# Zero-padding the query block of each head to 128 rows for the score matmuls, and an fp32 matmul in place of a cast and a bf16 one

## The chip, the cores and the metric

One Trainium2 chip, 8 cores, each on 4 of the 32 sequences. There is no traffic between the cores. The metric is device microseconds of the slowest core. The profile names the engines PE (matrix), PEld (its weight loads), DVE (vector), ACT (scalar), POOL (GpSimd) and SP (DMA issue).

## The reference, cut to what matters

```python
def attn(x, Wq, bq, Wk, bk, Wv, bv, Wo, bo):      # 16 heads of 64, S = 2048, D = 1024
    q, k, v = ((x @ W + b).reshape(B, S, 16, 64).transpose(0, 2, 1, 3)
               for W, b in ((Wq, bq), (Wk, bk), (Wv, bv)))
    scores = einsum('bhqd,bhkd->bhqk', q, k) / sqrt(64)
    out = einsum('bhqk,bhkd->bhqd', softmax(scores, -1), v)
    return out.transpose(0, 2, 1, 3).reshape(B, S, D) @ Wo + bo

def ffn(x, w_gate, w_up, w_down):                 # hidden 3072, weights int * 1/127
    return (silu(x @ wg.T) * (x @ wu.T)) @ wd.T

x = x + layernorm(attn(layernorm(x), ...))
x = x + layernorm(ffn(layernorm(x), ...))
```

x is (32, 2048, 1024) in fp32.

## The kernel before

The program first casts and transposes the weights, and then goes through four sequences, one after the other. Each sequence has three stages: (A) layer norm, and the K, Q and V projections; (B) attention; (C) the feed-forward part in two halves. The change touches stage B alone.

In stage B, `K_fm` and `Q_fm` hold K and Q transposed: 128 partitions are two heads of 64, and head h lies in column block hc = h // 2 at partitions hr = 64 * (h % 2) onward. The unit of work is one head for one group of 512 queries: 64 units a sequence, unit u being group g = u // 16 and head h = u % 16. A unit walks the 2048 keys in 16 tiles of 128, taken as 8 pairs:

- two score matmuls (L479): weights are 64 rows x 128 keys of K, the moving operand is 64 rows x 512 queries of Q. They write a pair of PSUM banks; two such pairs alternate.
- one exponential on ACT (L486) over the 128x1024 pair, into one half of `Ebuf`. It is called exp below, exp0 to exp7 in a unit.
- two PV matmuls (L459): weights are 128 keys x 65 columns of V (64, and one of ones that sums the row), the moving operand is `Ebuf`. They run one pair late: PE's order is score 0, score 1, PV 0, score 2, PV 1, ..., score 7, PV 6, PV 7.

Then comes the normalisation. `plan_epi1` copies the row of sums to `srow` (L500, DVE; "the sums copy" below). `plan_epi2` takes Ln and Exp of it on ACT (L509, L511, giving `rs`), casts `rs` to bf16 (L514, DVE), spreads it over 64 partitions by a one-row matmul with a row of ones (L516, PE; "the spread"), copies the result out (L525, DVE) and multiplies the PV result by it into `attn_fm` (L527, DVE). `plan_epi2` of unit u-1 is emitted after the matmuls of unit u, and `plan_epi1` of u behind that. `rs_bf` lies in `gbf`, a buffer that the feed-forward stage uses too.

The order of everything is that of the code: `Plan.step` appends to a list, each engine runs its own steps of that list in order, and semaphore waits are written by hand. In units with index 1 to 8 of groups 1 to 3, half an output tile of the group before follows: `plan_otile` with 8 full matmuls (L546), a one-row bias matmul (L552) and a copy on ACT (L556). After each second half, in units of even index, `plan_ctile` follows: two layer norms of one 128-token tile, a chain that goes to and fro between DVE (L310 to L329, L575, L580, L587) and ACT (L323, L326). Of the 63 places where one unit follows another in a sequence, 12 hold half an output tile, 12 hold the other half and a `plan_ctile`, and 39 neither. The last group's output tiles come at the end of the stage.

Of the kernel before, what the change touches and what calls it, by code (L numbers as in the profile page):

```python
# [17 lines left out]
QSC = 1.0 / 127.0  # L18
SPREAD_OPROJ = True
PVLAG = True  # L20
E4BF16 = True


class PSem:
# [66 lines left out]
def build_program(truncate=None, truncate_at=None, debug_scratch=False):  # L91
# [43 lines left out]
    K_fm = AR[:, 0:16384]  # L135
    Q_fm = AR[:, 16384:32768]
# [33 lines left out]
    Wo_s = Wx[:, 8192:16384]  # L170
    gbf = sb("gbf", [128, 1024], BF16)
    rs_bf = gbf[0:1, 0:512]
    bstat = sb("bstat", [128, 12], F32)
    mvt = sb("mvt", [128, 2], F32)
    rst = sb("rst", [128, 1], F32)
# [13 lines left out]
    p = Plan()  # L189
# [3 lines left out]
    def rw(*names):  # L193
# [12 lines left out]
           inc=[(g_ev, 1)])  # L206
    p.step("gpsimd", lambda e: e.iota(coli, [[1, 128]], channel_multiplier=0,
                                      allow_small_or_imprecise_dtypes=True),
           inc=[(g_ev, 1)])
    p.step("vector", lambda e: e.tensor_tensor(ident_bf, ident_f, coli, ALU.is_equal),  # L210
           wait=[g_ev], inc=[(g_ev, 1)])
    p.step("vector", lambda e: e.tensor_tensor(ident_f, ident_f, coli, ALU.is_equal),
           wait=[g_ev], inc=[(g_ev, 1)])
# [4 lines left out]
    for nm, src, dstT in (("bq", BQ, bqT), ("bk", BK, bkT)):  # L218
        p.step("sync", lambda e, src=src: e.dma_start(
            out=bstg, in_=src.rearrange("(c p) -> c p", p=128)),  # L220
            wait=[(g_mm, g_mm.count)], inc=[(g_ld, 16)], tag=f"ldb_{nm}")
        p.step("tensor", lambda e: e.transpose(ps[:, 0:8], bstg, ident_f[0:8, 0:8]),
               wait=[g_ld, g_ev], inc=[(g_mm, 1)], tag=f"trb_{nm}")
        p.step("vector", lambda e, dstT=dstT: e.tensor_copy(dstT, ps[:, 0:8]),
               wait=[g_mm], inc=[(g_ev, 1)], tag=f"evb_{nm}")
    for nm, src, dst in (("bv", BV, bv_bf), ("bo", BO, bo_bf)):
        p.step("sync", lambda e, src=src: e.dma_start(
            out=brow, in_=src.rearrange("(a d) -> a d", a=1)),
            wait=[(g_ev, g_ev.count)], inc=[(g_ld, 16)], tag=f"ldr_{nm}")
        p.step("vector", lambda e, dst=dst: e.tensor_copy(dst, brow),  # L230
               wait=[g_ld], inc=[(g_ev, 1)], tag=f"cvr_{nm}")

    for nm, src in (("wq", WQ), ("wk", WK), ("wv", WV), ("wo", WO)):
        p.step("gpsimd", lambda e, src=src: e.dma_start(
            out=fstage[:, 0:8192], in_=src.rearrange("(c p) o -> p c o", p=128)),
            wait=[(g_st, g_st.count)], inc=[(g_ldg, 16)], tag=f"cast_{nm}")
        p.step("sync", lambda e, nm=nm: e.dma_start(
            out=wbf[nm].rearrange("(c p) o -> p c o", p=128), in_=fstage[:, 0:8192]),
            wait=[g_ldg], inc=[(g_st, 16)], tag=f"park_{nm}")
    for nm, src, dst in (("wg", WG, wg_bf), ("wu", WU, wu_bf), ("wd", WD, wd_bf)):  # L240
        p.step("gpsimd", lambda e, src=src: e.dma_start(
            out=fstage, in_=src.rearrange("(c p) o -> p c o", p=128)),
            wait=[(g_st, g_st.count)], inc=[(g_ldg, 16)], tag=f"cast_{nm}")
        p.step("sync", lambda e, dst=dst: e.dma_start(
            out=dst.rearrange("(c p) o -> p c o", p=128), in_=fstage),
            wait=[g_ldg], inc=[(g_st, 16)], tag=f"park_{nm}")

    for nm, srcs, dstT in (("wg", wg_bf, wgT_bf), ("wu", wu_bf, wuT_bf)):
        for c in range(8):
            for hg in range(6):  # L250
# [3 lines left out]
                    wait=[(g_st, g_st.count)], inc=[(g_lds, 16)], tag=f"xp_{nm}{c}_{hg}")  # L254
# [20 lines left out]

    lxs = [p.sem("lxa"), p.sem("lxb"), p.sem("lxc")]
    vns = p.sem("vns")
    lxi = [p.sem("lxia"), p.sem("lxib")]
    cs_x1 = [p.sem("csx1a"), p.sem("csx1b")]
    cs_l3 = [p.sem("csl3a"), p.sem("csl3b")]  # L280
# [22 lines left out]
    for s in range(NSEQ):  # L303
# [163 lines left out]
        def plan_unit(u):  # L467
            g, h = u // 16, u % 16
            hc, hr = h // 2, 64 * (h % 2)
            for jp in range(8):  # L470
                P = u * 8 + jp
                pr = P % 2
                for j in (2 * jp, 2 * jp + 1):
                    w = []
                    if j % 2 == 0:
                        w.append((sxp, max(0, sxp.count - 1)))
                    if u == 0 and j == 0:
                        w += builds_done
                    p.step("tensor", lambda e, j=j, pr=pr, hc=hc, hr=hr, g=g: e.matmul(  # L479
                        ps[:, 1024 * pr + 512 * (j % 2): 1024 * pr + 512 * (j % 2) + 512],  # L480
                        K_fm[hr:hr + 64, hc * 2048 + j * 128: hc * 2048 + (j + 1) * 128],
                        Q_fm[hr:hr + 64, hc * 2048 + g * 512: hc * 2048 + (g + 1) * 512],
                        start=True, stop=True),
                        wait=w, inc=([(smm, 1)] if j % 2 == 1 else []),
                        tag=f"s{s}sT{u}_{j}")
                p.step("scalar", lambda e, pr=pr: e.activation(  # L486
                    Ebuf[:, 1024 * pr:1024 * (pr + 1)],
                    ps[:, 1024 * pr:1024 * (pr + 1)], AF.Exp, scale=0.125),
                    wait=[(smm, smm.count), (pvm, pvm.count)],
                    inc=[(sxp, 1)], tag=f"s{s}xp{u}_{P}")  # L490
                if PVLAG:
                    if jp >= 1:
                        plan_pv_pair(u, jp - 1, sxp.count - 1)
                else:
                    plan_pv_pair(u, jp, sxp.count)
            if PVLAG:
                plan_pv_pair(u, 7, sxp.count)
# [345 lines left out]
```

How the kernel before makes its waits and increments, by code:

```python
            def body(eng):  # L66
                waited = {}
                for si, (engine, fn, waits, incs, tag) in enumerate(steps):
                    if engine != engine_name:
                        continue
                    for sm, val in waits:
                        if val > 0 and waited.get(id(sm), -1) < val:
                            eng.wait_ge(sm.handle, val)
                            waited[id(sm)] = val
                    inst = fn(eng)
                    self.emitted[si] = inst
                    if incs:
                        assert inst is not None, f"step {tag} needs inst for incs"
                        for sm, amt in incs:
                            inst = inst.then_inc(sm.handle, amt)
```

## Time and profile before

| what | us |
|---|---|
| median of 2 runs | 11290.91 |
| their range | 11266.82 to 11315.01 |
| the profiled execution's own time | 11263.55 |
| its span on the slowest core (core 7) | 11262.0 |
| spans of the eight cores | 11164.9 to 11262.0 |

The span runs from the first to the last instruction of the slowest core, and all rows below are of that core. Busy shares are means over stages with different limits, so the stage that the change touches has to be read by itself. PEclk is the clock that TensorE was granted, as a share of 2.4 GHz: 0.50 is 1.2 GHz, 1.00 is 2.4 GHz.

### The profile page before, as it was taken

To read this page: it belongs to the slowest core of one execution; us is meant where nothing else is said; L and a number is where in the kernel's file an instruction comes from. 1 tells how busy PE (TensorE), PEld (TensorE's weight loads), DVE (VectorE), ACT (ScalarE), POOL (GpSimd) and SP (SyncE) were. 2 spreads that over 40 slices of the span, in tenths; PEclk is the share of its full clock that TensorE was granted. 3 is DMA by queue.
4 is the path that set the end of the run, shared out by engine and by line. 5 is a ranking of instruction groups with operands and counts; after the bars stand their busy time and mean duration, and the time that the engine had idled before them with its cause. 6 is when DMAs were issued, how large, how long until landed. Compare 5 with 4: busy or idle time off the path is not lost.

```text
span 11262.0 us, 71264 instructions; the slowest of 8 cores (11164.9 to 11262.0 us)
## 1 busy us (share of the span) xinstructions
PE 7816.7 (69%) x22530; PEld 2125.4 (19%) x22530; DVE 3190.8 (28%) x5389; ACT 2811.4 (25%) x3601; POOL 335.0 (3%) x401
## 2 busy tenths in 40 slices
PE   0079888675648888866647988866575888886755
PEld 0031111122222111122212111112222211111222
DVE  0141221233352111234344122123335311122334
ACT  0005444300002444410000544430000244441000
POOL 0000000000000000000000000000000000000000
PEclk9985555587876555578877555558677655556767
DMA  9630000112131000012123000011213100001121
GB/s 194 155 109 0 19 14 14 47 40 77 53 101 49 10 14 14 19 57 63 56 79 101 0 19 19 10 47 45 71 42 107 54 10 12 17 19 54 40 71 62
DMA packets 300509, 558.30 MB, mean 50 GB/s; under 512 B 159842, under 2 KB 159858, under 8 KB 300148
## 3 DMA queue, kind: packets, MB, share of 16 engines
q0 software_dynamic: 81072, 287.34, 9.1%
q1 hardware_dynamic: 141508, 247.52, 6.6%
q10 hardware_dynamic: 77568, 18.89, 0.9%
q8 instruction: 195, 3.19, 0.1%
q14 instruction: 166, 1.36, 0.0%
HBM read 415.25 MB, written 130.02 MB: 48 GB/s over the span
## 4 chain that ended last, share of the span: by engine, by line
PE 57%; DVE 15%; DMA 10%; issue 7%; ACT 6%; ACTq 2%; SPq 2%; POOL 1%; DVEq 0%; POOLq 0%
PE ps L479 14%; PE ps L459 14%; PE ps L726 7%; PE ps L732 7%; DMA arena<-wdT_bf 4%; PE ps L397 4%; PE ps L679 4%; PE ps L546 4%; DVE arena L693 3%; PE ps L421 2%; DMA x1st<-x_s 2%; ACT rs L511 1%; ACT brow L509 1%; PE ps L516 1%; SPq L654 1%
## 5 line engine op out<-in xcount | busy, mean ns | idle before, releaser
L486 ACT ACTIVATE Ebuf<-ps 128x1024 bf16<-128x1024 f32 x2048 | 2069.1, 1023 | 2195.6 <-PE ps L479 2194.8
L459 PE MATMUL ps<-Ebuf,arena 128*65 128x512 bf16 x4096 | 2154.8, 628 | 655.9 <-ACT Ebuf L486 550.8
L726 PE MATMUL ps<-arena 128*128 128x512 bf16 x3072 | 1311.7, 427 | 1138.9 <-DMA arena<-wdT_bf 710.7
L479 PE MATMUL ps<-arena 64*128 64x512 bf16 x4096 | 2017.4, 606 | 6.5 <-DVE arena L434 6.5
L732 PE MATMUL ps<-arena 128*128 128x512 bf16 x3072 | 1305.2, 425 | 0.0
L514 DVE CAST gbf<-rs 1x512 bf16<-1x512 f32 x256 | 106.2, 415 | 3802.4 <-ACT rs L511 3802.4
L679 PE MATMUL ps<-arena 128*128 128x512 bf16 x3072 | 807.4, 394 | 184.0 <-DVE arena L693 147.8
L739 ACT ACTIVATE gbf<-ps 128x512 bf16<-128x512 f32 x384 | 229.3, 597 | 2823.9 <-PE ps L732 2823.8
L744 DVE SCALAR_TENSOR_TENSOR arena<-ps,gbf 128x512 bf16<-128x512 f32 x384 | 265.6, 692 | 2239.3 <-ACT gbf L739 2239.3
L362 PE MATMUL ps<-ident_bf,ln3st 128*128 128x128 bf16 x512 | 104.5, 266 | 1091.9 <-DVE ln3st L348 1026.1
L693 DVE SCALAR_TENSOR_TENSOR arena<-ps,arena 128x1024 f32<-128x1024 f32 x704 | 829.0, 1219 | 54.9 <-PE ps L679 26.6
L459 PEld LDWEIGHTS ps<-Ebuf,arena 128*65 128x65 bf16 x4096 | 382.7, 143 | 2357.3 <-issue 2357.3
L726 PEld LDWEIGHTS ps<-arena 128*128 128x128 bf16 x3072 | 329.7, 107 | 1628.5 <-issue 1419.6
L479 PEld LDWEIGHTS ps<-arena 64*128 64x128 bf16 x4096 | 295.5, 109 | 1471.6 <-issue 1458.8
L546 PE MATMUL ps<-Wx,attn_fm 128*128 128x512 bf16 x1024 | 435.3, 602 | 92.9 <-ACT o_tm L556 85.6
L397 PE MATMUL ps<-ln_bl,Wx 128*128 128x512 bf16 x2048 | 479.2, 398 | 13.2 <-DVE ln_bl L365 9.0
L732 PEld LDWEIGHTS ps<-arena 128*128 128x128 bf16 x3072 | 327.4, 107 | 439.6 <-issue 226.9
L679 PEld LDWEIGHTS ps<-arena 128*128 128x128 bf16 x3072 | 265.0, 98 | 711.9 <-issue 551.4
L705 POOL DMA_DIRECT2D arena<-wgT_bf x96 | 87.2, 909 | 8887.1 <-PE ps L479 5368.7
L516 PE MATMUL ps<-gbf,ones_bf 1*64 1x512 bf16 x256 | 153.5, 600 | 198.2 <-DVE gbf L514 198.2
L323 ACT ACTIVATE o_tm<-o_tm,epsv 128x1 f32<-128x1 f32 x64 | 18.8, 294 | 1056.7 <-DVE o_tm L316 1056.7
L362 PEld LDWEIGHTS ps<-ident_bf,ln3st 128*128 128x128 bf16 x512 | 52.2, 104 | 1146.3 <-issue 1137.7
(74 smaller groups left out, 3635.4 us busy)
## 6 DMA issues: line engine op xcount, KB each, us to landing
xin<-x SPq DMA_DIRECT2D x128, 512.0 KB, 4.2
arena<-wgT_bf POOLq DMA_DIRECT2D x96, 512.0 KB, 4.9
arena<-wuT_bf POOLq DMA_DIRECT2D x96, 512.0 KB, 5.8
arena<-wdT_bf POOLq DMA_DIRECT2D x96, 512.0 KB, 6.3
Wx<-wk_bf POOLq DMA_DIRECT2D x32, 1024.0 KB, 6.2
Wx<-wq_bf POOLq DMA_DIRECT2D x32, 1024.0 KB, 6.0
Wx<-wv_bf POOLq DMA_DIRECT2D x32, 1024.0 KB, 6.1
x_s<-x1st SPq DMA_DIRECT2D x64, 512.0 KB, 2.7
```

The lines of the kernel that those rows point to most:

```text
L397: p.step("tensor", lambda e, wsl=wsl, di=di, do4=do4, bk_i=bk_i: e.matmul(bank(bk_i), Wslot[wsl][:, di * 512 + do4 * 128: di * 512 + (do4 ...
L459: p.step("tensor", lambda e, j=j, pr=pr, u=u, h=h: e.matmul(ps[0:65, 2048 + 512 * (u % 2): 2048 + 512 * (u % 2) + 512], Vaug[:, j * 1040 + ...
L479: p.step("tensor", lambda e, j=j, pr=pr, hc=hc, hr=hr, g=g: e.matmul(ps[:, 1024 * pr + 512 * (j % 2): 1024 * pr + 512 * (j % 2) + 512], K_ ...
L486: p.step("scalar", lambda e, pr=pr: e.activation(Ebuf[:, 1024 * pr:1024 * (pr + 1)], ps[:, 1024 * pr:1024 * (pr + 1)], AF.Exp, scale=0.125 ...
L516: p.step("tensor", lambda e: e.matmul(ps[0:64, 3072:3584], ones_bf[0:1, 0:64], rs_bf[0:1, :], start=True, stop=True), wait=[epi], inc=[(ep ...
L546: p.step("tensor", lambda e, di=di, t4=t4, n=n, gb=gb: e.matmul(bank(7), attn_fm[:, gb + di * 512 + t4 * 128: gb + di * 512 + (t4 + 1) * 128],
L679: p.step("tensor", lambda e, c=c, n=n, tt=tt, hsl=hsl, fsl=fsl, dbk=dbk: e.matmul(bank(dbk + n), h_sfm[hsl][:, c * 1024 + tt * 128: c * 10 ...
L693: p.step("vector", lambda e, at=at, dbk=dbk: e.scalar_tensor_tensor(at, bank2(dbk), QSC, at, ALU.mult, ALU.add), wait=[(fdm, fdm.count)], ...
L726: p.step("tensor", lambda e, di=di, c=c, u2=u2, fsl=fsl, gbk=gbk: e.matmul(bank(gbk), wgT_s[fsl][:, di * 256 + c * 128: di * 256 + (c + 1) ...
L732: p.step("tensor", lambda e, di=di, c=c, u2=u2, fsl=fsl, ubk=ubk: e.matmul(bank(ubk), wuT_s[fsl][:, di * 256 + c * 128: di * 256 + (c + 1) ...
L739: p.step("scalar", lambda e, gbk=gbk, gsl=gsl: e.activation(gbf[:, gsl * 512:(gsl + 1) * 512], bank(gbk), AF.Silu, scale=QSC), wait=[(fmm, ...
L744: p.step("vector", lambda e, ubk=ubk, gsl=gsl, hsl=hsl, c=c, u2=u2: e.scalar_tensor_tensor(h_sfm[hsl][:, c * 1024 + u2 * 512: c * 1024 + ( ...
```

## The change

Before each unit, DVE now fills one half of `gbf` (under the name `Q_z`, 128x512 bf16, two halves that alternate) with the Q block of the unit's head in its own 64 partitions and zeros in the other 64. The score matmul takes all 128 rows of K's block, both heads of it, as weights, and `Q_z` as its moving operand. The zeros cancel the other head, so the result is the same. Since `gbf` is taken, the reciprocal is spread by a matmul on fp32 data, `rs` against `ones64f`, and the cast to bf16 goes.

```diff
-E4BF16 = True
+E4BF16 = False
...
+    Q_z = gbf
...
+    qz = p.sem("qz")
...
         def plan_unit(u):
             g, h = u // 16, u % 16
             hc, hr = h // 2, 64 * (h % 2)
+            hrc = 64 - hr
+            z = u % 2
+            wz = [(smm, max(0, smm.count - 8))]
+            if u == 0:
+                wz += builds_done
+            p.step("vector", lambda e, z=z, hrc=hrc: e.memset(
+                Q_z[hrc:hrc + 64, z * 512:(z + 1) * 512], 0.0),
+                wait=wz, inc=[(qz, 1)], tag=f"s{s}qz0_{u}")
+            p.step("vector", lambda e, z=z, hr=hr, hc=hc, g=g: e.tensor_copy(
+                Q_z[hr:hr + 64, z * 512:(z + 1) * 512],
+                Q_fm[hr:hr + 64, hc * 2048 + g * 512: hc * 2048 + (g + 1) * 512]),
+                inc=[(qz, 1)], tag=f"s{s}qz1_{u}")
             for jp in range(8):
...
                     if j % 2 == 0:
                         w.append((sxp, max(0, sxp.count - 1)))
-                    if u == 0 and j == 0:
-                        w += builds_done
-                    p.step("tensor", lambda e, j=j, pr=pr, hc=hc, hr=hr, g=g: e.matmul(
+                    if jp == 0 and j % 2 == 0:
+                        w.append((qz, qz.count))
+                    p.step("tensor", lambda e, j=j, pr=pr, hc=hc, z=z: e.matmul(
                         ps[:, 1024 * pr + 512 * (j % 2): 1024 * pr + 512 * (j % 2) + 512],
-                        K_fm[hr:hr + 64, hc * 2048 + j * 128: hc * 2048 + (j + 1) * 128],
-                        Q_fm[hr:hr + 64, hc * 2048 + g * 512: hc * 2048 + (g + 1) * 512],
+                        K_fm[:, hc * 2048 + j * 128: hc * 2048 + (j + 1) * 128],
+                        Q_z[:, z * 512:(z + 1) * 512],
                         start=True, stop=True),
```

The order on DVE, in a unit with neither output tile nor `plan_ctile`, before; L500 is the sums copy of one unit, the others normalise that unit, a unit later:

```order
L500 COPY brow<-ps 1x512 [waits pvm0,epi]
L514 CAST gbf<-rs 1x512 [waits epi]
L525 COPY rsb<-ps 64x512 [waits epi]
L527 SCALAR_TENSOR_TENSOR attn_fm<-ps,rsb 64x512 [waits epi]
L500 COPY brow<-ps 1x512 [waits pvm0,epi]
```

The same place after; L514 is now the sums copy, L477 and L480 make the next unit's padded block, L539 and L541 are the former L525 and L527:

```order
L514 COPY brow<-ps 1x512 [waits pvm0,epi]
L477 MEMSET gbf 64x512 [waits smm0]
L480 COPY gbf<-arena 64x512
L539 COPY rsb<-ps 64x512 [waits epi]
L541 SCALAR_TENSOR_TENSOR attn_fm<-ps,rsb 64x512 [waits epi]
L514 COPY brow<-ps 1x512 [waits pvm0,epi]
```

The two steps for unit u+1 stand behind the sums copy of unit u, which is itself behind the normalisation of unit u-1; the cast is gone.

The order on PE where one unit follows another, before; L459 is PV 7, L516 the spread, L479 the first two score pairs of the next unit, and L459 its PV 0:

```order
L459 MATMUL ps<-Ebuf,arena 65x512 [waits sxp]
L459 MATMUL ps<-Ebuf,arena 65x512
L516 MATMUL ps<-gbf,ones_bf 64x512 [waits epi]
L479 MATMUL ps<-arena 128x512 x4
L459 MATMUL ps<-Ebuf,arena 65x512 [waits sxp,epi]
```

The same place after; L461 is PV, L535 the spread, L493 the score matmuls:

```order
L461 MATMUL ps<-Ebuf,arena 65x512 [waits sxp]
L461 MATMUL ps<-Ebuf,arena 65x512
L535 MATMUL ps<-rs,ones64f 64x512 [waits epi]
L493 MATMUL ps<-gbf,arena 128x512 [waits qz]
L493 MATMUL ps<-gbf,arena 128x512 x3
L461 MATMUL ps<-Ebuf,arena 65x512 [waits sxp,epi]
```

The order of the matmuls is the same; the first score matmul of a unit has a new wait, for DVE.

The order on DVE at the end of a `plan_ctile`, after the change; L331 and L601 are the last two steps of its second layer norm (L329 and L587 before), and before the change L514, the cast, came next:

```order
L331 SCALAR_TENSOR_TENSOR nmr<-mvt,rst 128x1 [waits ce]
L601 SCALAR_TENSOR_TENSOR ln3st<-x1st,rst,nmr 128x1024 [waits ce]
L477 MEMSET gbf 64x512 [waits smm0]
L480 COPY gbf<-arena 64x512
L539 COPY rsb<-ps 64x512 [waits epi]
```

The padded block for the next unit thus stands behind the whole chain of `plan_ctile`.

## Rows read from the trace of the kernel before

**Rows 1.** The page's chain of work that ended last, shares of the span by line.

```profile
PE ps L479 14%; PE ps L459 14%; PE ps L726 7%; PE ps L732 7%; DMA arena<-wdT_bf 4%; PE ps L397 4%; PE ps L679 4%; PE ps L546 4%; DVE arena L693 3%; PE ps L421 2%; DMA x1st<-x_s 2%; ACT rs L511 1%; ACT brow L509 1%; PE ps L516 1%; SPq L654 1%
```

**Rows 2.** Windows of the attention stages: busy us of each engine, PEclk, DMA share, GB/s.

```profile
836.00:2161.00 1325.00, 1117.16 (x2323) 203.94 (x2322) 238.86 (x381) 613.44 (x709) 0.95 (x2) 0.52 0.03 12
...
sum 5302.00, PE 4468.99 PEld 815.41 DVE 955.42 ACT 2453.97 POOL 3.92; mean PE 1117.25 PEld 203.85 DVE 238.85 ACT 613.49 POOL 0.98
```

**Rows 3.** Timeline of a plain unit: start us, busy us, engine, line, operation.

```profile
937.33 1.02 ACT L486 ACTIVATE Ebuf<-ps 128x1024 bf16<-128x1024 f32 x1 [0.93 <-PE ps L479]
...
938.95 0.63 ACT L511 ACTIVATE rs<-brow 1x512 f32<-1x512 f32 x1
939.68 0.41 DVE L514 CAST gbf<-rs 1x512 bf16<-1x512 f32 x1 [14.42 <-ACT rs L511]
...
940.24 0.60 PE L516 MATMUL ps<-gbf,ones_bf 1*64 1x512 bf16 x1 [0.71 <-DVE gbf L514]
...
940.77 1.88 PE L479 MATMUL ps<-arena 64*128 64x512 bf16 x4
...
942.52 0.69 DVE L500 COPY brow<-ps 1x512 f32<-1x512 f32 x1
...
943.35 1.03 PE L459 MATMUL ps<-Ebuf,arena 128*65 128x512 bf16 x2 [0.69 <-DVE brow L500]
...
944.32 1.03 PE L479 MATMUL ps<-arena 64*128 64x512 bf16 x2
...
955.27 1.02 ACT L486 ACTIVATE Ebuf<-ps 128x1024 bf16<-128x1024 f32 x1 [0.93 <-PE ps L479]
```

**Rows 4.** Timeline around two units with output tiles and one `plan_ctile`.

```profile
1202.21 1.02 ACT L486 ACTIVATE Ebuf<-ps 128x1024 bf16<-128x1024 f32 x1 [0.93 <-PE ps L479]
...
1224.10 1.02 ACT L486 ACTIVATE Ebuf<-ps 128x1024 bf16<-128x1024 f32 x1 [0.93 <-PE ps L479]
...
1240.43 1.28 DVE L587 SCALAR_TENSOR_TENSOR ln3st<-x1st,rst,nmr 128x1024 bf16<-128x1024 f32 x1
...
1253.18 1.02 ACT L486 ACTIVATE Ebuf<-ps 128x1024 bf16<-128x1024 f32 x1 [0.93 <-PE ps L479]
```

**Rows 5.** Windows of short stretches in attention, columns as in rows 2.

```profile
946.00:956.00 10.00, 10.00 (x21) 1.57 (x20) 0.00 (x0) 5.35 (x6) 0.00 (x0) 0.50 0.00 0
1205.70:1211.00 5.30, 5.30 (x14) 1.51 (x13) 2.05 (x3) 0.69 (x2) 0.00 (x0) 0.50 0.00 0
1227.60:1231.00 3.40, 3.40 (x9) 0.98 (x8) 2.05 (x3) 0.00 (x0) 0.00 (x0) 0.50 0.00 0
1231.00:1234.40 3.40, 1.43 (x6) 0.39 (x5) 1.50 (x3) 0.89 (x2) 0.00 (x0) 1.00 0.00 0
1234.50:1241.00 6.50, 0.00 (x0) 0.00 (x0) 4.89 (x8) 1.55 (x5) 0.00 (x0) 0.50 0.00 0
8870.00:8880.00 10.00, 8.25 (x30) 1.96 (x30) 0.00 (x0) 7.56 (x8) 0.00 (x0) 1.00 0.00 1
```

**Rows 6.** Timeline of the first unit of the last sequence.

```profile
8870.12 1.02 PE L479 MATMUL ps<-arena 64*128 64x512 bf16 x4 [1.60 <-DVE arena L434]
8870.80 1.94 ACT L486 ACTIVATE Ebuf<-ps 128x1024 bf16<-128x1024 f32 x2 [55.53 <-PE ps L479]
...
8872.49 0.60 PE L479 MATMUL ps<-arena 64*128 64x512 bf16 x2
8873.03 0.62 PE L459 MATMUL ps<-Ebuf,arena 128*65 128x512 bf16 x2
...
8879.50 1.02 ACT L486 ACTIVATE Ebuf<-ps 128x1024 bf16<-128x1024 f32 x1 [0.34 <-PE ps L479]
```

**Rows 7.** Groups of instructions: shapes, count, busy us, mean ns, idle before.

```profile
L514 DVE CAST gbf<-rs 1x512 bf16<-1x512 f32 x256 | 106.2, 415 | 3802.4 <-ACT rs L511 3802.4
...
L333 DVE MEMSET arena<- 128x16640 bf16 x4 | 55.7, 13925 | 513.6 <-issue 513.6
...
L214 DVE MEMSET ones_bf<- 1x128 bf16 x1 | 0.2, 165 | 0.0
```

## The prediction, made before the changed kernel was run

> **What bounds the kernel now.** I read the chain of waits first. Its two dearest lines are the score and the PV matmuls, 14% each [rows 1], so attention is where matmuls set the end. The windows by stage say how much that is: four attention stages like the one shown last 5302 us of the 11262 us span, PE is busy in 4469 us of them, ACT in 2454, and the mean granted clock is 0.52 [rows 2]. The other 5960 us are not touched by the change.
>
> The timeline of a plain unit (neither output tile nor `plan_ctile`) tells where its 17.94 us go, counted from exp7 to the next exp7 [rows 3]. exp7 starts at 0; the reciprocal is ready at 2.25; the cast runs from 2.35; the spread starts at 2.91, the score matmuls at 3.44; the sums copy ends at 5.88 and lets PV 0 go at 6.02; the next exp7 starts at 17.94. From PV 0 on PE runs without a break: 12 pairs of matmuls stand between PV 0 and exp7. Four score matmuls in a row take 1.88 us, of which the last one's 0.60 is its whole duration: 0.427 us apart. But a pair is 0.97 us (943.35 to 944.32), not 0.854: each change between the 64-row and the 128-row matmuls costs 0.12 us. 12 x 0.97 + 0.28 for the tail = 11.92, the rest of the unit.
>
> The windows then show the clock [rows 5]. In 946 to 956 PE is busy for all 10 us and is granted 0.50, its level of 1.2 GHz. A burst of 128x128 matmuls of an output tile fills 1227.6 to 1231.0, and from 1231 the clock is 1.00, 2.4 GHz; after 6.5 us without a matmul it is back at 0.50. A like burst at 1205.7 changes nothing. And where a sequence enters attention at 2.4 GHz, straight from the full projection matmuls, the old score and PV matmuls keep it for a unit (8870 to 8880, 1.00). So it isn't being busy that lifts the clock here: half-filled matmuls don't lift it, full ones do, and mixed work can hold it. At 2.4 GHz matmuls stand 0.213 us apart, a pair 0.54 (0.427 and the same 0.12), and the eight exps are 1.243 us apart ((8879.50 - 8870.80) / 7), near ACT's own 0.97 [rows 6].
>
> **The change part by part.** Everything is worked out on the profiled execution, 11263.55 us; the median of the runs is 27 us above it.
>
> *Full rows in the score matmuls.* 4096 matmuls of the same number and width, so at one clock none is longer. Two things may go. First, no 64-row matmul is left beside the 128-row PV ones: the 0.12 us per pair goes if it comes from the change of rows, and stays if PV's 65 columns cause it. Four matmuls of one shape show none, so I let it go: pairs of 0.854 at 1.2 GHz. At 2.4 GHz two exps took 2.486 us by the chain exp, PV, score, exp; without two changes 2.246, so 1.12 us an exp. Second, the clock: half the matmuls become full.
>
> The first is where a rule of the Trainium skill bears. TensorEngine Tiling, under Tiling Modes, says that switching the tiling mode, not just the tile, drains the engine, and lists no column mode wider than 64 other than the full one. By it the 0.12 us is the price of going between 64 and 128 rows and vanishes whole; the trace agrees in size (0.12 us per pair at either clock), but shows no 65-column matmul beside a 128-column one of 128 rows. If it stays, the sum is that of the third rival below.
>
> *Zeros and copy on DVE.* 256 memsets and 256 copies of 64x512. The long memset costs 13925 / 16640 = 0.84 ns an element, 0.43 us for 512 (bounds 0.165, a 1x128 memset, and 0.68, the 1x512 sums copy out of PSUM); the copy lies between 0.165 and the cast's 0.415, and I take 0.25 [rows 3, 7]. Both stand behind the sums copy of the unit before, and PE waits for them: they are wholly on the path. With 0.14 us to hand over (the sums copy's end at 943.21 to PV 0 at 943.35), that is 0.82 us from the sums copy to the first score matmul. Queued behind that matmul on PE is the whole next unit, and behind its scores ACT. Before, four score matmuls ran while DVE was still normalising; that cover goes. The wait of a sequence's first unit for the projections moves from PE to DVE, 4 x 0.82 us that I leave out.
>
> *The spread in fp32 and no cast.* The spread starts at 2.25 + 0.14 = 2.39 instead of 2.91. No fp32 matmul of this width is in the trace. An fp32 number holds two bf16 ones, so the product is between one pass and four: 0.21 to 0.85 us at 2.4 GHz, 0.43 to 1.71 at 1.2; I take four. Before, from the spread to the sums copy's end is 2.97 us with one pass of 0.43. So the sums copy ends at 2.39 + 2.97 - 0.43 + 0.85 = 5.78, and the score matmuls start at 6.60 (7.46 if the spread runs at 1.2 GHz), against 3.44.
>
> *What the clock does.* From PV 7 (1.02 + 0.14 + 0.43 = 1.6) to 6.60 PE does only the one-row spread. After such idle time the trace shows 0.50, so I let each plain unit start at 1.2 GHz. Of the two bursts one was granted 2.4 GHz 3.4 us after it began, one not by its end; I let the first 5 us of a unit's score and PV matmuls run at 1.2 GHz.
>
> *Plain units* (39 a sequence, 156 in all). First score 6.60. At 2.4 GHz exp0 starts 0.68 after the first of four score matmuls (8870.12 to 8870.80) [rows 6], at 1.2 GHz two spacings of 0.213 later, 1.11; PV 0 another 1.02 + 0.14 on: 2.27. In the 5 us to the rise 3.2 pairs of the 12 are done; 8.8 are left, 4.4 exps x 1.12 = 4.93; tail 0.28. exp7 at 6.60 + 5.0 + 4.93 + 0.28 = 16.8: 1.14 us less, 156 x 1.14 = 178 us.
>
> *Units with half an output tile* (48). 21.89 us before (1202.21 to 1224.10) [rows 4]. Now the burst runs on PE while DVE normalises and pads, and it fills the pause, so I let the clock stay up. At 2.4 GHz it is done in 2 us, before DVE is. Scores at 6.60, exp0 0.68 later, exp7 7 x 1.12 later: 15.1. 6.8 us less, 326 us.
>
> *Units with `plan_ctile`* (48). 29.08 us before (1224.10 to 1253.18). The last DVE step of the chain ended at 17.61; it moves by -0.52 (cast), +0.42 (spread) and -8 x 0.214 = -1.71 (output tile at 2.4 GHz), to 15.8. Before, the scores of the next unit were done by then and exp0 ran beside that step; now memset and copy come behind it: scores at 16.6, and 10.2 us more as in a plain unit, 26.8. 2.3 us less, 110 us.
>
> Sum: 178 + 326 + 110 = 614 us; 11263.55 - 614 = 10650 us. The late work in each unit is now DVE's chain at its start and ACT behind the score matmuls.
>
> **The rivals.**
>
> *The clock stays at 1.2 GHz* (slower). Half of the work is still the 65-column PV, or rows of zeros may not count. Then a plain unit's scores start at 7.46 and exp7 is 2.27 + 12 x 0.854 + 0.28 = 12.8 later: 20.26, 2.32 more, +362 us. Half-tile units: spread to 4.2, burst to 8.15, 20.95: 0.94 less, -45. `plan_ctile` units: 17.61 - 0.52 + 1.28 + 0.82 + 12.8 = 32.0, 2.9 more, +140. In all 11720 us. It decides in the plain unit: with the rise later than 8.3 us after the first score matmul, that unit is longer than before. Against it: the bursts of full matmuls did lift the clock, and PV has all 128 rows. TensorE: Matmul & The Clock Gate, in Part 1, says of the Trainium skill's clock gate that it follows how busy PE has lately been. Read as busy time alone, this change gives the clock nothing, which is this rival; the trace disagrees, with 10.00 of 10 us busy at 0.50.
>
> *The clock never falls between units.* Plain units are 6.60 + 0.68 + 7.84 = 15.1, 2.8 less: 440 in place of 178, 10390 us. For it: the spread now is longer. Against it: it has one row, and 3.3 us behind it are empty.
>
> *The 0.12 us per pair stays.* Exps 1.243 apart, cold pairs 0.97. Plain units 17.6 (-53 us), half-tile units 16.0 (-284), `plan_ctile` units 27.6 (-71): 408 us, 10856 us. For it: the weights still change from 128 to 65 columns.
>
> **How the numbers follow.** Forecast 0.69; clock stays 0.14; never falls 0.07; 0.12 us stays 0.10. The forecast's own range: the spread's price (one pass: -0.64 us in 204 units, -131; cold +0.86, +175), memset and copy (-0.35 to +0.42, some 100 either way), the rise (3.4 to 8.3 us moves a plain or `plan_ctile` unit by -0.55 to +1.14, -112 to +233). Together 10400 to 10950. The range goes from 10350, with the never-falling clock, to 11050, with the third rival and a late rise; the slow rival is left out above. About 2% (225 us) can be told from no change. Faster: 0.69, 0.07 and nearly all of the 0.10, less the forecast's late rises: 0.79. Slower: 0.14 less what half-tile bursts save there: 0.13. Same: 0.08.
>
> **What would show it.** Right: score and PV matmuls evenly 0.427 or 0.213 us apart; a clock of 0.50 at each plain unit's start and 1.00 in its second part; exps 1.0 to 1.2 us apart there; the first score matmul waiting for DVE's copy, 6 to 7.5 us after exp7; a spread of 1 us. Wrong: attention windows still at 0.52, exps 1.7 apart; score and PV pairs at 0.54 or 0.97; units with an output tile falling to 0.50 at their start; a memset or copy much over 0.5 us.

## The result, and the profile after

| what | before | after |
|---|---|---|
| median on one chip, us | 11331.06 (10 runs) | 10904.39 (11 runs) |
| ratio, 95% interval | | 0.9518 (0.9464 to 0.9572) |
| the profiled execution, us | 11263.55 | 10861.58 |

The change makes the kernel 4.8% faster; 10650 us was forecast (5.5% less), 10350 to 11050 the range. Some executions of every kernel here are disturbed on four or all of the cores and some per cent longer; the ratios leave them out, the medians don't, and the spans of cores given from here on are of undisturbed ones (11153 to 11195 us before and 10698 to 10720 after, in two executions of each).

The chain of waits by line, of after, against [rows 1]: the two matmul lines of attention fell from 14% each to 7% and 6%, and ACT's exp (L500) stands first.

```profile
ACT Ebuf L500 9%; PE ps L740 7%; PE ps L493 7%; PE ps L746 7%; PE ps L461 6%; DMA arena<-wdT_bf 5%; PE ps L399 4%; PE ps L693 4%; DVE arena L707 3%; PE ps L535 3%; PE ps L423 2%; DMA x1st<-x_s 2%; PE ps L560 2%; ACT rs L525 2%; ACT brow L523 1%
```

The windows of the attention stages of after (slowest core, 2), columns as in [rows 2]:

```profile
870.00:2112.00 1242.00, 798.91 (x2390) 237.66 (x2390) 263.08 (x452) 609.31 (x710) 3.15 (x4) 0.74 0.04 13
...
6094.00:7304.00 1210.00, 748.23 (x2389) 229.92 (x2387) 261.84 (x446) 605.70 (x710) 3.22 (x4) 0.80 0.04 14
...
sum 4885.00, PE 3062.41 PEld 929.66 DVE 1049.31 ACT 2428.90 POOL 13.53; mean PE 765.60 PEld 232.42 DVE 262.33 ACT 607.23 POOL 3.38
```

The four stages went from 5302 to 4885 us and the granted clock from 0.52 to between 0.74 and 0.81: the 417 us are all of the gain (402 us between the two profiled executions). PE is busy 1407 us less for the same score and PV matmuls. Core 5 of the same execution has 0.81 in its first stage too (840 to 2050), so the 0.74 of this core's first is not what the change does.

The timeline of a plain unit of after, against [rows 3]. exp7 is the second of the two exps that start at 6168.75, so it starts at 6169.67:

```profile
6168.75 1.94 ACT L500 ACTIVATE Ebuf<-ps 128x1024 bf16<-128x1024 f32 x2 [0.41 <-PE ps L493]
...
6171.29 0.63 ACT L525 ACTIVATE rs<-brow 1x512 f32<-1x512 f32 x1
6172.07 1.04 PE L535 MATMUL ps<-rs,ones64f 1*64 1x512 f32 x2 [0.64 <-ACT rs L525]
...
6174.79 0.69 DVE L514 COPY brow<-ps 1x512 f32<-1x512 f32 x1
6175.53 0.48 DVE L477 MEMSET gbf<- 64x512 bf16 x1
6176.04 0.29 DVE L480 COPY gbf<-arena 64x512 bf16<-64x512 bf16 x1
6176.48 1.86 PE L493 MATMUL ps<-gbf,arena 128*128 128x512 bf16 x4 [3.38 <-DVE gbf L480]
6177.65 1.94 ACT L500 ACTIVATE Ebuf<-ps 128x1024 bf16<-128x1024 f32 x2 [5.73 <-PE ps L493]
...
6179.75 1.06 PE L493 MATMUL ps<-gbf,arena 128*128 128x512 bf16 x2
6180.60 0.67 PE L461 MATMUL ps<-Ebuf,arena 128*65 128x512 bf16 x2
6180.96 1.94 ACT L500 ACTIVATE Ebuf<-ps 128x1024 bf16<-128x1024 f32 x2 [1.38 <-PE ps L493]
...
6183.30 1.94 ACT L500 ACTIVATE Ebuf<-ps 128x1024 bf16<-128x1024 f32 x2 [0.41 <-PE ps L493]
...
6185.65 1.94 ACT L500 ACTIVATE Ebuf<-ps 128x1024 bf16<-128x1024 f32 x2 [0.41 <-PE ps L493]
```

And the granted clock in it, columns as in [rows 5]:

```profile
6176.40:6180.50 4.10, 3.44 (x8) 1.11 (x9) 0.00 (x0) 1.94 (x2) 0.00 (x0) 0.50 0.00 0
6180.60:6187.80 7.20, 5.64 (x24) 1.94 (x23) 0.00 (x0) 6.03 (x7) 0.00 (x0) 0.99 0.00 0
```

The first score matmul starts 6.81 us after exp7, released by DVE's copy (L480). PE then runs at 1.2 GHz for 4.1 us and at 2.4 GHz from there. A pair of score matmuls and the pair of PV matmuls behind it start 0.85 us apart (6179.75 to 6180.60), twice 0.427: the 0.12 us of before is gone. From 6180.96 two exps take 2.345 us, 1.17 each. The next exp7 starts at 6185.65 + 0.92 = 6186.57, 16.90 us after this one; 17.94 before.

A unit with half an output tile (exp7 at 3831.47), then one with `plan_ctile`, then another half tile (from 3874.82), of after, against [rows 4]:

```profile
3831.47 1.02 ACT L500 ACTIVATE Ebuf<-ps 128x1024 bf16<-128x1024 f32 x1 [0.33 <-PE ps L493]
...
3838.38 1.02 PE L493 MATMUL ps<-gbf,arena 128*128 128x512 bf16 x4 [1.32 <-DVE gbf L480]
3839.12 1.94 ACT L500 ACTIVATE Ebuf<-ps 128x1024 bf16<-128x1024 f32 x2 [1.38 <-PE ps L493]
...
3846.27 1.94 ACT L500 ACTIVATE Ebuf<-ps 128x1024 bf16<-128x1024 f32 x2 [0.41 <-PE ps L493]
...
3861.66 1.28 DVE L601 SCALAR_TENSOR_TENSOR ln3st<-x1st,rst,nmr 128x1024 bf16<-128x1024 f32 x1
...
3863.95 1.87 PE L493 MATMUL ps<-gbf,arena 128*128 128x512 bf16 x4 [11.18 <-DVE gbf L480]
...
3868.92 1.06 PE L493 MATMUL ps<-gbf,arena 128*128 128x512 bf16 x2
...
3874.82 1.02 ACT L500 ACTIVATE Ebuf<-ps 128x1024 bf16<-128x1024 f32 x1 [0.41 <-PE ps L493]
...
3881.73 1.02 PE L493 MATMUL ps<-gbf,arena 128*128 128x512 bf16 x4 [1.33 <-DVE gbf L480]
...
3883.75 1.03 PE L461 MATMUL ps<-Ebuf,arena 128*65 128x512 bf16 x2 [1.00 <-ACT Ebuf L500]
...
3892.07 1.02 ACT L500 ACTIVATE Ebuf<-ps 128x1024 bf16<-128x1024 f32 x1 [0.41 <-PE ps L493]
```

The first half tile takes 15.72 us (the next exp7 is at 3846.27 + 0.92 = 3847.19): clock up from end to end. The second takes 17.25: its four score matmuls run at 2.4 GHz (1.02 us for four), but 2 us later PV does not (1.03 us for two). The `plan_ctile` unit takes 27.63; 29.08 before.

From the starts of all 2048 exps of a core come the distances from exp7 to exp7; the last column is forecast against mean, times the count:

| units | before, mean of core 7 | forecast | after, mean | after less forecast |
|---|---|---|---|---|
| plain, 156 | 17.92 | 16.8 | 17.15 | +54 us |
| half tile, 48 | 21.86 | 15.1 | 16.68 | +76 us |
| `plan_ctile`, 48 | 29.26 | 26.8 | 28.17 | +66 us |

The three make 196 of the 212 us by which the profiled execution is above the forecast. The means are of core 2; on cores 4 to 7 of the same execution they are 17.03 to 17.06, 16.51 to 16.68 and 27.89 to 27.98, still all above the forecast.

The groups of after, against [rows 7]:

```profile
L535 PE MATMUL ps<-rs,ones64f 1*64 1x512 f32 x512 | 278.5, 624 | 172.7 <-ACT rs L525 172.7
...
L477 DVE MEMSET gbf<- 64x512 bf16 x256 | 124.2, 485 | 28.2 <-issue 20.3 <-DVE arena L436 1.2
L480 DVE COPY gbf<-arena 64x512 bf16<-64x512 bf16 x256 | 73.7, 288 | 8.0
```

The fp32 spread is two matmuls per unit (512 for 256), 1.04 us together; memset and copy are 0.485 and 0.288 us.

### The profile page after: what moved, and what is told of

It is laid out like the page before. It is cut to its first block, busy times and chain, and to the rows that moved or that the text cites. A ratio compares the mean times of both kernels' runs of the same rounds, so it can differ in the third digit from the quotient of the medians.

```text
span 10860.0 us, 72294 instructions; the slowest of 8 cores (10752.6 to 10860.0 us)
## 1 busy us (share of the span) xinstructions
PE 6419.6 (59%) x22786; PEld 2241.5 (21%) x22786; DVE 3281.0 (30%) x5645; ACT 2782.3 (26%) x3601; POOL 334.6 (3%) x401
## 4 chain that ended last, share of the span: by engine, by line
PE 43%; DVE 16%; ACT 14%; issue 11%; DMA 11%; ACTq 2%; SPq 2%; POOL 1%; DVEq 0%; POOLq 0%
ACT Ebuf L500 9%; PE ps L740 7%; PE ps L493 7%; PE ps L746 7%; PE ps L461 6%; DMA arena<-wdT_bf 5%; PE ps L399 4%; PE ps L693 4%; DVE arena L707 3%; PE ps L535 3%; PE ps L423 2%; DMA x1st<-x_s 2%; PE ps L560 2%; ACT rs L525 2%; ACT brow L523 1%
## 5 line engine op out<-in xcount | busy, mean ns | idle before, releaser
L500 ACT ACTIVATE Ebuf<-ps 128x1024 bf16<-128x1024 f32 x2048 | 2037.4, 1022 | 1966.0 <-PE ps L493 1945.3
L493 PE MATMUL ps<-gbf,arena 128*128 128x512 bf16 x4096 | 1503.4, 469 | 1138.3 <-DVE gbf L480 1138.3
L740 PE MATMUL ps<-arena 128*128 128x512 bf16 x3072 | 1282.8, 418 | 1146.8 <-DMA arena<-wdT_bf 716.8
L461 PE MATMUL ps<-Ebuf,arena 128*65 128x512 bf16 x4096 | 1418.4, 432 | 534.4 <-ACT Ebuf L500 521.9
L746 PE MATMUL ps<-arena 128*128 128x512 bf16 x3072 | 1275.1, 415 | 0.0
L539 DVE COPY rsb<-ps 64x512 f32<-64x512 f32 x256 | 174.7, 683 | 3554.3 <-PE ps L535 3554.3
L693 PE MATMUL ps<-arena 128*128 128x512 bf16 x3072 | 791.1, 386 | 192.3 <-DVE arena L707 151.1
L707 DVE SCALAR_TENSOR_TENSOR arena<-ps,arena 128x1024 f32<-128x1024 f32 x704 | 828.8, 1218 | 49.5 <-PE ps L693 15.8
L493 PEld LDWEIGHTS ps<-gbf,arena 128*128 128x128 bf16 x4096 | 443.3, 113 | 1906.4 <-issue 1656.0
L461 PEld LDWEIGHTS ps<-Ebuf,arena 128*65 128x65 bf16 x4096 | 358.7, 121 | 1569.7 <-issue 1562.1
L399 PE MATMUL ps<-ln_bl,Wx 128*128 128x512 bf16 x2048 | 516.1, 420 | 14.0 <-DVE ln_bl L367 9.4
L535 PE MATMUL ps<-rs,ones64f 1*64 1x512 f32 x512 | 278.5, 624 | 172.7 <-ACT rs L525 172.7
L560 PE MATMUL ps<-Wx,attn_fm 128*128 128x512 bf16 x1024 | 311.0, 459 | 82.3 <-ACT o_tm L570 74.9
```

The lines of the kernel that those rows point to most:

```text
L399: p.step("tensor", lambda e, wsl=wsl, di=di, do4=do4, bk_i=bk_i: e.matmul(bank(bk_i), Wslot[wsl][:, di * 512 + do4 * 128: di * 512 + (do4 ...
L461: p.step("tensor", lambda e, j=j, pr=pr, u=u, h=h: e.matmul(ps[0:65, 2048 + 512 * (u % 2): 2048 + 512 * (u % 2) + 512], Vaug[:, j * 1040 + ...
L493: p.step("tensor", lambda e, j=j, pr=pr, hc=hc, z=z: e.matmul(ps[:, 1024 * pr + 512 * (j % 2): 1024 * pr + 512 * (j % 2) + 512], K_fm[:, h ...
L500: p.step("scalar", lambda e, pr=pr: e.activation(Ebuf[:, 1024 * pr:1024 * (pr + 1)], ps[:, 1024 * pr:1024 * (pr + 1)], AF.Exp, scale=0.125 ...
L535: p.step("tensor", lambda e: e.matmul(ps[0:64, 3072:3584], ones64f[0:1, :], rs[0:1, :], start=True, stop=True), wait=[epi], inc=[(epi, 1)] ...
L560: p.step("tensor", lambda e, di=di, t4=t4, n=n, gb=gb: e.matmul(bank(7), attn_fm[:, gb + di * 512 + t4 * 128: gb + di * 512 + (t4 + 1) * 128],
```

## The experiments

The theory is the forecast's: full score rows lift the clock and end the 0.12 us; DVE's padding and the pause that it makes give part of it back. Its rivals: another part of the change brings the gain; zeros matter; or the pause is harmless.

**The score on 64 rows again.** All else as after.

```diff
-                        K_fm[:, hc * 2048 + j * 128: hc * 2048 + (j + 1) * 128],
-                        Q_z[:, z * 512:(z + 1) * 512],
+                        K_fm[hr:hr + 64, hc * 2048 + j * 128: hc * 2048 + (j + 1) * 128],
+                        Q_z[hr:hr + 64, z * 512:(z + 1) * 512],
```

> The changed kernel with all its DVE steps and waits, but the score matmuls take only the 64 rows of their own head, as before the change. Theory: the rows are what lifts the clock and what ends the 0.12 us between unlike matmuls; without them the new waits are all cost. Granted clock of the attention stages 0.52 again. A plain unit: first score at 7.7 us, PV 0 2.35 later, 12 pairs of 0.97 and 0.28: 22.0 us instead of 17.94, +630 us over 156 units; with half-tile units (+0.7) and plan_ctile units (+4.7) about 12100 us, 8% over the kernel before. Rival, the clock rises for another reason (the longer pauses, the fp32 spread): clock about 0.79, only the 0.12 us per pair back, about 11000 us.

12215.49 us median, ratio to before 1.0724 (1.0599 to 1.0849). The sum of its attention windows, and two rounds of score and PV pairs inside a unit:

```profile
sum 6159.00, PE 4780.48 PEld 855.97 DVE 1047.44 ACT 2455.04 POOL 2.36; mean PE 1195.12 PEld 213.99 DVE 261.86 ACT 613.76 POOL 0.59
```

```profile
4017.69 1.03 PE L493 MATMUL ps<-gbf,arena 64*128 64x512 bf16 x2
4018.65 1.06 PE L461 MATMUL ps<-Ebuf,arena 128*65 128x512 bf16 x2
...
4019.65 1.03 PE L493 MATMUL ps<-gbf,arena 64*128 64x512 bf16 x2
```

Each of its four windows has a clock of 0.52, as before the change, and two score and two PV matmuls take 1.96 us (4017.69 to 4019.65), 0.98 a pair. Both effects hang on the rows of the score matmuls, and without them the padding costs 7%: 22.0 us in the mean plain unit. The rest of the change brings nothing by itself. What no run separates is the 64 rows from the going to and fro between 64 and 128 rows: here they come and go together.

**The spread in bf16.** After, with the cast into spare bytes of `brow` and the bf16 spread.

```diff
-E4BF16 = False
+E4BF16 = True
...
-    rs_bf = gbf[0:1, 0:512]
+    rs_bf = brow[0:1, 512:768].bitcast(BF16)
```

> The changed kernel, with the cast to bf16 and the bf16 spread back (the bf16 reciprocal lies in the spare half of brow). Theory: the two sides of this edit nearly cancel. In the changed kernel the fp32 spread starts 2.40 us after exp7 and the sums copy ends 3.41 us later, at 5.81. With the cast the spread starts at 2.91, and from there to the end of the sums copy it is the 2.97 us of the kernel before less 0.21 for a pass at 2.4 GHz, so 5.67: 0.14 us earlier in 204 units, about 30 us less (10690 against 10720), no more than 0.5%. Rival: the fp32 spread is the dear part of the new chain; then 0.6 us and more in each of 252 units, 150 us less or better.

10735.64 us median, ratio 0.9534 (0.9442 to 0.9626), beside 0.9518 of after: no difference, as expected. A cast with a bf16 spread takes nearly as long as an fp32 spread without a cast.

**Padding a unit ahead.** Memset and copy for unit u+1 are issued in unit u, ahead of its normalisation; `plan_pad` holds the two steps.

```diff
+            qzn = qz.count
+            if u < 63:
+                plan_pad(u + 1)
             for jp in range(8):
...
-                        w.append((qz, qz.count))
+                        w.append((qz, qzn))
```

> The changed kernel with memset and copy for unit u+1 issued on DVE in unit u ahead of its normalisation. Theory: the chain of normalisation, sums copy, memset and copy in front of the first score matmul (first score 6.81 us after exp7) is what each plain unit pays and why its clock falls. First score then comes right behind the spread, at about 3.5 us, PV 0 waits for the sums copy until 5.95, the clock stays at 2.4 GHz or falls for part of a unit: plain units 12.9 (clock stays) to 14.8 us (falls) instead of 17.05, plan_ctile units about 3 us less; 9850 to 10150 us in all. Rival: only memset and copy themselves are on the path (0.87 us in 204 units): 10540 us. Rival: they are hidden: 10720.

**No padding, both heads' scores summed.** The moving operand is Q as it lies, 128 rows, so each score is the sum of two heads' and the output is another; memset and copy go.

```diff
-                        Q_z[:, z * 512:(z + 1) * 512],
+                        Q_fm[:, hc * 2048 + g * 512: hc * 2048 + (g + 1) * 512],
```

> The changed kernel without memset and copy: the score matmul takes all 128 rows of K and of Q as they lie, so that it adds up the scores of two heads (the padding is left out, and the wait for it). Theory: time depends on rows and waits, not on the zeros; the same times as with the early padding, 9850 to 10150 us, within 1% of it. Rival: rows of zeros count for less than rows of data in the clock or draw less; then the clock of the attention stages here differs from that of the kernel with early padding, and the time by 2% or more.

Early padding: 10296.75 us median, ratio 0.9005 (0.8894 to 0.9116), spans of 10050.9 to 10115.0 us. Both heads: 10282.16 us, 0.8962 (0.886 to 0.9065), spans of 10057.9 to 10087.3. Both lie in the range expected and they agree, so the zeros themselves cost nothing in clock or time; where DVE makes them does. The third attention window of the first is 1048 us long (1210 of after):

```profile
5808.00:6856.00 1048.00, 753.43 (x2338) 236.76 (x2384) 261.06 (x443) 604.47 (x709) 0.94 (x2) 0.81 0.05 16
```

A plain unit of it, with exp7 at 5902.30:

```profile
5905.67 1.04 PE L499 MATMUL ps<-gbf,arena 128*128 128x512 bf16 x4
...
5908.25 1.03 PE L461 MATMUL ps<-Ebuf,arena 128*65 128x512 bf16 x2 [1.54 <-DVE brow L520]
```

The scores start 3.37 us after exp7 instead of 6.81, yet the clock still falls: the first PV matmuls take 1.03 us for two. They wait for the sums copy (L520) as well. Of the 3.4 us saved, 2.6 stay in the mean plain unit (14.51 us against 17.15).

**Work of no use in the pause.** After, with full matmuls into a free bank in units without an output tile: first 14 behind the spread.

```diff
+            if 1 <= u < 63 and not (u >= 16 and 1 <= u % 16 <= 8):
+                for k in range(14):
+                    p.step("tensor", lambda e: e.matmul(
+                        bank(7), K_fm[:, 0:128], K_fm[:, 0:512],
+                        start=True, stop=True),
```

> The changed kernel, with 14 matmuls of 128x128 by 512 columns, whose result nobody reads, behind the spread of each plain unit, about 3 us of work at 2.4 GHz in a pause of 3.4. Theory: part of what the pause costs is that the clock falls in it and the unit's first 4 to 5 us run at 1.2 GHz. With the pause filled the clock stays at 1.00 in plain units and the unit is 6.81 + 0.68 + 7 x 1.17 = 15.7 us instead of 17.05: 1.35 us in 156 units, about 210 us less than the changed kernel, near 10510 us, although PE has more to do. Rival: the pause costs only its own length; then the same as the changed kernel (10720), or more, if the filling delays the scores.

Largely a miss: 11083.19 us median; spans of 10625.4 to 10660.0 us, some 65 us under after, where 210 were expected. Windows of one plain unit (core 5), before the pause, in it, and behind it:

```profile
906.00:910.00 4.00, 3.19 (x14) 0.90 (x11) 0.00 (x0) 3.60 (x4) 0.00 (x0) 1.00 0.02 6
...
912.50:916.00 3.50, 3.50 (x10) 1.25 (x10) 2.83 (x5) 0.00 (x0) 0.00 (x0) 0.54 0.00 0
916.00:920.00 4.00, 2.91 (x13) 1.16 (x12) 0.00 (x0) 1.94 (x2) 0.00 (x0) 0.98 0.00 0
```

The clock had fallen by the time the added matmuls began. They ran at 0.54 and were still running when DVE's copy was done, so the scores came 1.2 us late (exp0 7.81 us after exp7's end, 6.5 to 6.6 in the few units where the clock was up), and a higher clock after that gave back little more than this: most such units take 16.9 us, the few take 15.6 to 15.7. So, with `range(8)` in place of `range(14)`, and after itself beside it:

> The changed kernel itself, to stand beside the next one on one chip. 10700 to 10900 us; plain units 17.0 us from one exp7 to the next (first exp 7.0 us after exp7's end, eight exps 10.05 us).

> The changed kernel, with 8 full 128x128 matmuls of no use (into a free PSUM bank) behind the spread in the units that hold no output tile, where 14 were tried before. The 14 still ran at 1.2 GHz for most of their length and ended 1.2 us after DVE's copy, so they pushed the first score matmul back by about what the higher clock then gave. 8 take 3.4 us at 1.2 GHz and should end with DVE's copy. Theory: what the fall of the clock costs a plain unit is its first scores and exps at half speed; with the clock up within 1 us of the first score matmul a unit takes about 16.0 us instead of 17.0, the total is some 150 us (1.4%) below the changed kernel. Rival: added matmuls lower the granted level in other places (matmuls of the feed-forward part more than 5% longer), so the total is that of the changed kernel or above.

A second miss. After itself: 11061.38 us median, spans of 10706.0 to 10732.2 us. With 8: 10987.92 us median, ratio 0.9553 (0.9513 to 0.9593), spans of 10675.1 to 10704.1: some 30 us less, where 150 were expected. The mean clock rose (0.82 to 0.84), the time hardly fell; the mean plain unit takes 16.8 us for 17.05. A plain unit of it (core 5):

```profile
912.43 1.90 PE L627 MATMUL ps<-arena 128*128 128x512 bf16 x8
...
915.88 1.02 PE L493 MATMUL ps<-gbf,arena 128*128 128x512 bf16 x4 [1.54 <-DVE gbf L480]
...
917.90 1.03 PE L461 MATMUL ps<-Ebuf,arena 128*65 128x512 bf16 x2 [1.00 <-ACT Ebuf L500]
```

Here the added matmuls and the scores run at 2.4 GHz (eight in 1.90 us), and the fall comes behind the first scores instead (PV: 1.03 us for two). It had only moved. Then with 3 ahead of the spread and 11 behind it:

> The changed kernel, with 3 full matmuls of no use ahead of the spread and 11 behind it in the units that hold no output tile, so that PE has work nearly all the way from PV 7 to the first score matmul. With 8 behind the spread alone, the fall of the clock did not go: it only came later, about 1 us after the first score matmul, and unit time stayed at 17.0 us. In the few units where the clock was up throughout, first scores and exps took 6.5 us of gap and 9.1 us of exps, 15.6 us. Theory: the fall belongs to the pause as a whole, and a unit in which it is filled from both sides keeps 1.00; most plain units then take 15.6 us, 156 x 1.4 = 220 us less than the changed kernel, about 10500. Rival: one stretch of one-row matmul and waiting is enough for a fall, wherever work is put around it: units stay at 17 us and the total at that of the changed kernel, 10700.

10905.75 us median; spans of 10552.0 to 10578.9 us, some 140 us under after, where 220 were expected. A plain unit of it (slowest core, 4), with exp7 at 3442.76:

```profile
3444.36 0.81 PE L621 MATMUL ps<-arena 128*128 128x512 bf16 x3
3445.16 1.04 PE L535 MATMUL ps<-rs,ones64f 1*64 1x512 f32 x2
3446.13 2.55 PE L633 MATMUL ps<-arena 128*128 128x512 bf16 x11
...
3449.67 1.02 PE L493 MATMUL ps<-gbf,arena 128*128 128x512 bf16 x4 [1.00 <-DVE gbf L480]
...
3457.56 1.94 ACT L500 ACTIVATE Ebuf<-ps 128x1024 bf16<-128x1024 f32 x2 [0.41 <-PE ps L493]
```

The first score matmul is 6.91 us after exp7, as in after, but the unit takes 15.72 us (to 3457.56 + 0.92 = 3458.48). 79 of the 156 plain units take 15.5 to 15.8 us, 57 take 16.5 to 17.6; the mean is 16.16. That isolates the fall: with everything else in place, in one and the same kernel, it costs about 1.4 us, 17.1 against 15.7.

**The normalisation in mid-unit.** Before, with the scores on 64 rows as they were, Ln, Exp and cast of unit u-1 behind pair 2 of unit u, and spread, copy and multiply behind pair 4:

```diff
+                    if u >= 1 and jp == 2:
+                        plan_epi2a(u - 1)
+                    if u >= 1 and jp == 4:
+                        plan_epi2b(u - 1)
```

> The kernel before (64-row scores, cast and bf16 spread), with the normalisation of the unit before moved into the middle of the unit: Ln, Exp and cast behind the third exp, the spread and its two DVE steps behind the fifth. Theory: taking the pause between units away shortens a 64-row kernel too, but cannot lift its clock. PE runs through at 1.2 GHz: 16 pairs of 0.97 and 0.55 for the spread, 16.1 us instead of 17.94; some 470 us less than the kernel before, near 10800 us, granted clock of the attention stages still 0.52 to 0.55. Rival: the pauses are what holds the clock down; then clock 0.9 and more, units of 11 us and 9800 us.

10818.51 us median; spans of 10669.3 to 10714.2 us, where after has 10698 to 10720. So the order alone is worth as much as the change, at nearly the old clock (0.57 or 0.58 in each attention window). Two stretches of it (slowest core, 2), the length of a plain unit, and a unit with half an output tile from exp7 to exp7:

```profile
950.00:967.08 17.08, 16.18 (x34) 2.82 (x33) 2.47 (x4) 9.10 (x10) 0.00 (x0) 0.50 0.00 0
1224.93:1241.22 16.29, 13.51 (x42) 3.45 (x42) 2.47 (x4) 9.56 (x11) 0.00 (x0) 0.81 0.00 0
```

In the plain unit PE is busy for the 16.1 us that were expected and waits for exps in the other 0.9; the clock is 0.50. The mean plain unit takes 17.08 us for 17.92. Half-tile units gain far more, 16.6 us in the mean for 21.86: in them the clock is up most of the time (0.81), with 64-row scores. That was not expected.

**Both together.** The same order on the changed kernel, with early padding and the bf16 spread; then also with `plan_ctile`'s layer norms cut in three and spread over the next unit (behind pairs 1 and 6).

> Full-row scores with early padding, cast and bf16 spread, and the normalisation of the unit before in the middle of the unit. Theory: with no pause between units the clock stays at 2.4 GHz and ACT becomes the bound: a plain unit is 8 exps of 1.0 to 1.17 us, 1.33 for Ln and Exp and about 1 us between units, 11 to 11.5 us instead of 14.2 with early padding alone; half-tile units 13, plan_ctile units 21.5; about 9480 us in all. Rival: Ln, Exp and the spread in the middle stall PE as long as they did between units; then no better than early padding alone, 10116 us.

> As the one before, and the two layer norms of plan_ctile are spread over the unit that follows: statistics where they were, the first Ln and Exp and their DVE steps behind the second exp, the second Ln and Exp behind the seventh. Theory: in plan_ctile units ACT waits 8 us for DVE, in order, before the next unit's exps; spread out, these units cost as much as half-tile units: 8 us less in 48 units, about 390 us less, near 9090 us. Rival: ACT still waits for DVE in the new places, or DVE delays the sums copy and with it PV 0; then less than half of that.

The first: 9809.43 us median, ratio 0.8509 (0.8257 to 0.876, a wide interval from two executions of each kernel), spans of 9573.8 to 9618.8 us; 9480 was expected, so the gain is there and smaller. Most plain units take 12.05 us, at a clock of 1.00. What was not counted lies between its third exp (955.02) and the fourth (957.18):

```profile
955.02 1.02 ACT L506 ACTIVATE Ebuf<-ps 128x1024 bf16<-128x1024 f32 x1 [0.51 <-PE ps L499]
...
955.94 0.61 ACT L530 ACTIVATE brow<-brow 1x512 f32<-1x512 f32 x1
...
956.64 0.63 ACT L532 ACTIVATE rs<-brow 1x512 f32<-1x512 f32 x1
957.18 1.90 ACT L506 ACTIVATE Ebuf<-ps 128x1024 bf16<-128x1024 f32 x2
```

These two are 2.16 us apart, others 1.17: Ln and Exp of the normalisation now sit between the exps on ACT. From exp0's start to exp7's end a plain unit takes 10.73 us; units of after that stay at 2.4 GHz take 9.08. The second: 9456.03 us median; spans of 9253.0 to 9273.3 us, some 340 us under the first (390 expected of this step), `plan_ctile` units 16.5 us instead of 23.2. It is the fastest kernel here.

## Why the prediction was right

- **The clock is lifted by full rows**: right, by the runs with 64 rows (0.52, slower than before) and with 128 (0.74 to 0.81). TensorE: Matmul & The Clock Gate, in Part 1, has the Trainium skill's gate follow how busy PE has been; the trace disagrees as far as busy time goes. In the run with the normalisation in mid-unit PE is busy for 16.18 of a plain unit's 17.08 us at a clock of 0.50; in the plain unit of after shown it is busy for 10.74 of 16.90 us, and the clock is 0.80 over the unit. Once up, the clock can stay up with 64-row scores, as the half-tile units of that run show (0.81).
- **The 0.12 us a pair goes**: right, at both clocks; the third rival falls. At 2.4 GHz a PV pair and the score pair behind it start 0.43 us apart (6182.13 and 6182.56), before the change 0.52 (8874.42 and 8874.94). By the Trainium skill's TensorEngine Tiling, Tiling Modes, a change of mode drains the engine; the trace agrees, with 0.12 us a pair between 64 and 128 rows and none between 128 and 65 columns. The Trainium skill states no price there, so the size is the trace's alone.
- **The chain on DVE**: right, but a little short. The spread started at 2.40 us (forecast 2.39), the sums copy ended at 5.81 (5.78), the first score came at 6.81 (6.60). Memset and copy took 0.77, not 0.68, and the handovers between the three steps and PE 0.23, not 0.14. The four passes assumed for the fp32 spread fit: 1.04 us against 0.37 to 0.40 of a bf16 one, three times 0.213 more.
- **The clock in a plain unit**: right. It falls in the pause and rises 4.1 us after the first score matmul (5 forecast). One row was read loosely: [rows 5] has 0.50 for the whole 6.5 us from 1234.5, and PE's last matmul ended at 1232.4, so there the fall came some 2 us into the rest and not after 6.5. The rival that it never falls is shown wrong for after, and its price right in kind: 15.7 us where it is made true, 15.1 forecast.
- **The pace at 2.4 GHz**: mis-sized, 1.17 us an exp for 1.12. Two exps lost 0.14 us (2.486 to 2.345), where I let both changes of mode, 0.24, go from the chain. With the later first score this is more than the earlier rise gives back: 17.15 for 16.8.
- **Half-tile units**: the step that failed is "it fills the pause, so I let the clock stay up". In 18 of 48 it does or nearly so, and they take 15.7 to 16.1 us (15.1 forecast, without the later first score and the slower pace). The other 30 take 16.9 to 18.0 us; in the one shown the fall comes behind the first scores. The run with 8 added matmuls shows the same in plain units: filling one side of the pause moves the fall.
- **`plan_ctile` units**: DVE's last step ended 15.75 us after exp7 (15.8 forecast), the scores began at 16.76 (16.6). From there to exp7 I took the 10.2 us of a plain unit; 10.87 it was in the unit shown, where the score matmuls at 3868.92, 5 us behind the first, still run at 1.2 GHz.

What stays open: when in a unit the fall and the rise come was read and not explained, and no run changes it by itself. The mean `plan_ctile` unit of 28.17 us against 27.63 in the one shown lies mostly in core 2's first stage (27.5 to 30.0 us there, mean 28.78); on core 5, whose clock in that stage is 0.81, the mean there is 27.83. Whether 64 rows as such, or the changes between 64 and 128 rows, kept the old clock down is open as well.

## What to carry to other kernels

Before a matmul is made fuller for the clock, ask what prepares its operand: here the padding stood behind the normalisation on DVE, held up the first score of a plain unit by 3.4 us, and in the pause the clock that it was to lift fell again; issued a unit earlier it cost next to nothing (spans as without any padding). Look first for work on the path that can go elsewhere: the order of the normalisation alone brought the old kernel what the padding brought, and the two together, with the padding made early, more than either. A higher mean clock is not a shorter time: where a fall is only moved, the clock's mean goes up and the units stay nearly as long as they were.

## What the runs showed of the hardware that was not expected

- An fp32 matmul with one row of 512 is two matmuls in the trace, 1.04 us together at 2.4 GHz and 1.94 at 1.2 GHz (in the run with 64 rows); a bf16 one is 0.40 us at 2.4 GHz.
- A matmul half of whose moving rows are zeros lifts the clock as one full of data does: 0.81 in the third attention window with zeros and with both heads, 753 and 758 us of PE.
- PE at work around a pause does not keep the clock through it: work on one side moved the fall (16.8 us a unit for 17.05), work on both sides kept it away in about half of the units (79 of 156 at 15.5 to 15.8 us).
